# A two-layer graph and feed-forward kernel: rows of two layers turned by transposing transfers instead of TensorE, VectorE's order in the linear layer, and two broadcasts moved

## What is computed

```python
x = x + _L0_gnn_ref(_layernorm(x), edge_weight, L0_gnn_bias, edge_index)       # layer 0: W built from edges; x @ W.T + bias
x = x + _L0_ffn_ref(_layernorm(x)[None], wg, w1, b1, w2, b2)[0]                # 8 experts, 2 for each row
x = x + _L1_gnn_ref(_layernorm(x), edge_index, L1_gnn_W, L1_gnn_b)             # linear layer, then a normalised sum over edges
x = x + _L1_ffn_ref(_layernorm(x)[None], L1_ffn_w1, L1_ffn_w2)[0]              # quantised feed-forward, 4096 hidden
```

## Time and profile before

| what | value |
|---|---|
| median of 3 runs | 1263.97 us |
| the profiled execution | 1262.48 us, of which the span is 1260.5 us |
| layer 0, first to last product | 149.3 to 263.5 us |
| linear layer, first product to last h | 613.4 to 728.9 us |
| TensorE's granted clock over the span | 0.947 of full speed |
| busy share: TensorE, VectorE, ScalarE | 84%, 63%, 38% |

### The profile page before, as it was taken

One profiled execution on the slowest core, in us unless ns is written; L12 is line 12 of the kernel. 1 busy time (PEld: TensorE's weight loads), 2 busy tenths in 40 slices (PEclk: granted clock), 3 DMA queues, 4 the chain that ended last, 5 costly groups with the idle time before them and its releaser, 6 DMA issues.

```text
span 1260.5 us, 20122 instructions
## 1 busy us (share of the span) xinstructions
PE 1063.4 (84%) x7645; PEld 593.5 (47%) x7645; DVE 788.6 (63%) x1082; ACT 481.3 (38%) x552; POOL 163.5 (13%) x215
## 2 busy tenths in 40 slices
PE   1777699974699999982699988888999999999998
PEld 1666344444456555551344444444444444444444
DVE  7998677678255555564677568888837444444431
ACT  3388434443344454451222223433223333333331
POOL 5200323311111110002312001111100000000000
PEclk9898799977699999996799989999999999999999
DMA  4466244363666766643422065666200000000000
GB/s 166 137 247 222 74 159 169 134 230 108 197 230 248 250 249 236 220 167 108 134 67 67 1 199 185 203 198 197 87 1 1 17 18 17 17 17 17 17 17 29
DMA packets 51803, 159.28 MB, mean 126 GB/s; under 512 B 12329, under 2 KB 12651, under 8 KB 47647
## 3 DMA queue, kind: packets, MB, share of 16 engines
q1 hardware_dynamic: 42143, 136.10, 30.8%
q0 software_dynamic: 9600, 22.36, 5.8%
HBM read 137.78 MB, written 20.65 MB: 126 GB/s over the span
## 4 chain that ended last, share of the span: by engine, by line
PE 56%; DVE 20%; issue 9%; DMA 7%; ACT 6%; POOL 1%; DVEq 1%; ACTq 0%; SPq 0%; POOLq 0%
PE ps L1045 11%; PE ps L1070 11%; PE ps L957 8%; PE ps L975 7%; PE ps L864 6%; PE ps L1027 4%; DVE fq L1900 4%; DVE stats L1444 2%; DMA fnat_a<-in_L_ffn_w 2%; DVE xn L1585 2%; DVE x L1848 1%; PE ps L931 1%; ACT xh L1187 1%; DMA gx<-xs_d,tok_i 1%; DVE w1l L1740 1%
## 5 line engine op out<-in xcount | busy, mean ns | idle before, releaser
L1045 PE MATMUL ps<-w1q,xqt 128*128 128x512 fp8e4 x640 | 139.7, 379 | 13.1 <-ACT xqt L1333 13.1
L1070 PE MATMUL ps<-w2q,hqt 128*128 128x512 fp8e4 x640 | 143.0, 379 | 8.7 <-ACT hqt L1342 8.7
L1935 DVE TENSOR_REDUCE hm<-hf 128x1 f32<-128x512 f32 x80 | 54.3, 685 | 93.5 <-ACT hf L1337 93.5
L1045 PEld LDWEIGHTS ps<-w1q,xqt 128*128 128x128 f16 x640 | 61.9, 98 | 87.7 <-issue 14.5
L1070 PEld LDWEIGHTS ps<-w2q,hqt 128*128 128x128 f16 x640 | 61.1, 98 | 78.6 <-issue 10.2
L1337 ACT ACTIVATE hf<-ps,fs 128x512 f32<-128x512 f32 x80 | 54.9, 687 | 91.0 <-PE ps L1045 91.0
L957 PE MATMUL ps<-xdh,w1h 128*128 128x314 f16 x256 | 77.6, 303 | 3.5 <-DVE w1l L1740 2.7
L957 PE MATMUL ps<-xdh,w1l 128*128 128x314 f16 x256 | 77.0, 301 | 0.0
L957 PE MATMUL ps<-xdl,w1h 128*128 128x314 f16 x256 | 76.8, 300 | 0.0
L644 POOL TENSOR_TENSOR rtmp<-mv,consts 128x1 f32<-128x1 f32 x40 | 12.7, 318 | 456.4 <-DVE mv L1449 456.4
L1342 ACT ACTIVATE hqt<-ps 128x1024 f16<-128x1024 f16 x40 | 39.8, 1022 | 68.3 <-PE ps L1052 68.3
(11 more groups left out here) (280 smaller groups left out, 2331.1 us busy)
## 6 DMA issues: line engine op xcount, KB each, us to landing
abs_in<-in_L_ffn_w SPq DMA_DIRECT2D x32, 1024.0 KB, 4.8
wstage<-in_L_ffn_w SPq DMA_DIRECT2D x32, 1024.0 KB, 11.9
fnat_a<-in_L_ffn_w SPq DMA_DIRECT2D x48, 512.0 KB, 4.4
eo_d<-eo SPq DMA_DIRECT2D x16, 512.0 KB
bias_b<-in_L_ffn_w SPq DMA_DIRECT2D x16, 512.0 KB, 4.1
xs_d<-xs_all SPq DMA_DIRECT2D x10, 512.0 KB, 4.3
out_x<-out_t SPq DMA_DIRECT2D x9, 512.0 KB, 2.6
b2b<-in_L_ffn_b SPq DMA_DIRECT2D x8, 512.0 KB
```

What stands on the lines that cost most here:

```text
L1045: last = mm(ps[:, n % 4, :], xqt[:, u, k, :], w1q[:, k, n * 512:(n + 1) * 512], start=(k == 0), stop=(k == KD - 1))
L1070: last = mm(ps[:, 4 + h, :], hqt[:, k, :], w2q[:, k, h * 512:(h + 1) * 512], start=(k == 0), stop=(k == KF - 1))
L1935: last = v.tensor_reduce(hm[:, u, n:n + 1], hf[:, u, n * 512:(n + 1) * 512], AX.X, ALU.max, apply_absolute_value=True)
```

## The change

1. **Turning by transfer.** In layer 0 and the linear layer tiles 2 to 9 (`by_transfer`) are no longer turned by TensorE. SP waits for `xh` and `xl` of the tile and stores both to a buffer in device memory, `xt_d`, in runs of 256 bytes (`rows_out`). Once the product of tile n-2 is done, and both stores and the transposing transfer before have landed, SP issues one transposing transfer of 512 KB into `xt` (`rows_turned`), which holds what were `xth` and `xtl`. TensorE waits for that (`wait_turned`). For these tiles TensorE's 16 transposes, ScalarE's copy `xth` and VectorE's copy `xtl` are gone. The routing stage still turns on TensorE.
2. **Written out.** The loops of these two stages on SP, TensorE, ScalarE and VectorE are written out instead of looped.
3. **VectorE's order in the linear layer.** The rest `hs_l` of tile i-1 now stands in iteration i, after `xn` of tile i+2; the two additions are split around `xl`.
4. **Broadcasts.** The linear layer's `bias_b` is issued before the stores `xs_d`, and no longer beside the last stores of the experts. `b2b` waits until the three gathers of expert 0 have landed; the loads of expert 1's weights stand behind it.

```diff
+        xt_d = nc.dram_tensor("xt_d", [2, 2 * KD * P, P], F16).ap()
...
+        FIRST = 2
+        def by_transfer(n):
+            return not R_MOE <= n < R_LIN1 and n % NT >= FIRST
...
+            def rows_out(n):
+                u = n % 2
+                sp.wait_ge(s_xh, n + 1)
+                sp.wait_ge(s_xl, n + 1)
+                for a, part in enumerate(parts(n, u)):
+                    sp.dma_start(xt_d[u].rearrange("(a k p) c -> a p k c", a=2, p=P)[a],
+                                 part.rearrange("p (k c) -> p k c", c=P)).then_inc(s_xrow, 16)
+            def rows_turned(n):
+                u = n % 2
+                sp.wait_ge(s_mm, n)
+                sp.wait_ge(s_xrow, 32 * moved(n) + 32)
+                if moved(n) > 0:
+                    sp.wait_ge(s_xt, 16 * moved(n))
+                sp.dma_start(xt[:, u, :, :, :].rearrange("p a k c -> p (a k c)"), xt_d[u], transpose=True).then_inc(s_xt, 16)
+            def transfers(r, i):
+                if by_transfer(r + i + 1) and i + 1 < NT:
+                    rows_turned(r + i + 1)
+                if i + 2 < NT:
+                    rows_out(r + i + 2)
...
+            sp.wait_ge(s_biased, NT)
+            sp.dma_start(bias_b[:, :], gb_in.partition_broadcast(P)).then_inc(s_bias, 16)
...
             sp.wait_ge(s_xstore, 16 * NT)
+            for s in range(3):
+                sp.wait_ge(s_g[s], 16)
             sp.dma_start(b2b[:, :], b2_in[0].partition_broadcast(P)).then_inc(s_b2, 16)
...
-            sp.dma_start(bias_b[:, :], gb_in.partition_broadcast(P)).then_inc(s_bias, 16)
+            for i in range(NT):
+                transfers(R_LIN1, i)
...
+            def wait_turned(n):
+                if by_transfer(n):
+                    pe.wait_ge(s_xt, 16 * moved(n) + 16)
+                else:
+                    pe.wait_ge(s_xth, turned(n) + 1)
+                    pe.wait_ge(s_xtl, turned(n) + 1)
...
+                for i in range(NT):
+                    if i + 1 < NT and not by_transfer(r + i + 1):
+                        transposes(r + i + 1, 1 - i % 2)
+                    body(i, i % 2)
...
+                if i + 2 < NT:
+                    norm(R_LIN1, i + 2, u)
+                if i > 0:
+                    rest_of_row(i - 1)
+                if i + 3 < NT:
+                    mixed(i + 3, 0)
+                if i + 2 < NT:
+                    low(R_LIN1 + i + 2, u)
+                if i + 3 < NT:
+                    mixed(i + 3, 1)
+                    mixed_statistics(i + 3)
```

More of the change, by code:

```diff
@@ L492, in _ @@
             sp.dma_start(wg32[:, :, :], wg_in.rearrange("(k p) e -> p k e", p=P)).then_inc(s_wg, 16)
-            with sp.Fori(0, 8) as j:
-                for u in range(2):
-                    sp.wait_ge(s_abs, 2 * j + u + 1)
-                    sp.dma_start(abs_in[:, u, :], f2_pieces[2 * j + u]).then_inc(s_absin[u], 16)
+            def rows_out(n):
[18 more added lines that the diff above has]
+            for i in range(NT):
+                if i < KD:
+                    for u in range(2):
+                        sp.wait_ge(s_abs, 2 * i + u + 1)
+                        sp.dma_start(abs_in[:, u, :], f2_pieces[2 * i + u]).then_inc(s_absin[u], 16)
+                transfers(R_GNN0, i)
             w1v = w1_in.rearrange("e (g k p) h -> e g p k h", g=2, p=P)
@@ L842, in transposes @@
                 pe.wait_ge(s_xh, n + 1)
[L843 to L844 removed]
+                if n > 0:
+                    pe.wait_ge(s_xth, turned(n))
                 for k in range(KD):
@@ L866, in product, with normalised @@
                 last.then_inc(s_mm, 1)
[L868 removed]
+            def normalised(r, body):
                 transposes(r, 0)
[L872 to L877 removed]
+                for i in range(NT):
+                    if i + 1 < NT and not by_transfer(r + i + 1):
+                        transposes(r + i + 1, 1 - i % 2)
+                    body(i, i % 2)
             pe.wait_ge(s_built, 1)
@@ L1602, in normalised @@
                 copy_low(r, 0)
-                def step(i, u):
-                    if not last_of(i, NT):
+                for i in range(NT):
+                    u = i % 2
+                    if i + 1 < NT and not by_transfer(r + i + 1):
                         dve.wait_ge(s_mm, r + i + 1)
                         copy_low(r + i + 1, 1 - u)
-                    if not last_of(i, NT, 2):
+                    if i + 2 < NT:
                         norm(r, i + 2, u)
```

101 lines of the change are left out of this document (56 added, 45 removed).

## The result

The changed kernel takes 1251.6 us at the median of its runs (1248.45 to 1256.98) against 1263.97 us before; the ratio of the two is 0.9894, with a 95% interval of 0.9868 to 0.992. That is 12 us less, inside the range of 1235 to 1263, but only six tenths of the 20 us that were forecast, and 1.6 us outside the forecast's own stretch of 1235 to 1250: it lies where the prediction had put rivals 3 and 2. The profiled executions differ by 1262.48 - 1251.82 = 10.7 us.

What follows compares the result with a forecast made beforehand. Stages of different limits alternate: 56% of the chain TensorE, 20% VectorE, 7% transfers. Terms -10.7 - 2 - 7 - 0.5 = -20.2 us took 1262.5 to 1242.3 as profiled, 1243.8 on the median; forecast 1243 us, range 1235 to 1263.

Steps and rivals of the forecast that it cites:

- rival 3: Third gather before the experts: slow by itself, so only 2 of the 7 us come; 1248 us, chance 0.08.
- rival 2: Layer 0: transfers late behind the loads, period 12.9 us, linear layer keeps its gain; 1257 us, chance 0.15.
- Linear layer, -10.7 predicted: Linear layer: without transposes TensorE becomes the bound at 10.36 us a tile, ending at 718.2 instead of 728.8.
- VectorE's two waits: Linear layer: VectorE waits for ScalarE, 1.59 us for hs_h and 1.12 for xh a tile; both were to go.
- Price of the transfer: Both layers: one transposing transfer of 512 KB was taken to land in 6 us.
- Neither bound: Length of one transposing transfer: at least 4.1 us from small pieces, at most 18.8 us from the mean packet.
- Rival 1: Both layers: transfers longer than a product, slower; 1370 us at 18.8 us each, point of decision about 12; chance 0.17.
- Layer 0, -2 predicted: Layer 0: writing out gives 1.9 us, removed transposes give nothing in the loop; 2 us less in all.
- it just fits: Layer 0: transfer lands about 12 us behind xl, behind two loads, against room of 12.2 us.
- the room of 12.2: Layer 0: longest latency from xl without delay, two VectorE periods less a product, 2 x 11.29 - 10.36.
- b2b and weights behind the gathers, -7 predicted: Third gather of gx: without the broadcasts it lands after the median 7.3 us instead of 14.76, less 0.5.
- bias_b, -0.5 predicted: Experts' last stores: bias_b no longer issued behind them gives 0.5 us, bounds 0 and 2; its new place costs nothing.

Runs made afterwards that it cites:

- the square: Four kernels compared on the linear layer: before 115.7 us, new VectorE order without transfers 111.8, transfers with old order 105.5, both 104.5.
- e3: Changed kernel, all transfers kept, with VectorE's linear-layer order put back as before: 1250.87 us, ratio 0.9903 to before.
- e7: Against e1, each transposing transfer of the linear layer made twice, the second after the first landed: 1268.0 us, ratio 1.0037 to before.
- e1: Changed kernel with layer 0 back on TensorE's transposes, still written out; transfers only in the linear layer: 1246.55 us, ratio 0.9875 to before.
- e6: Changed kernel with b2b issued as before, ahead of the gathers' end, so expert 1's weights early too: 1254.14 us, ratio 0.9942 to before.
- e1 to e3: e1, e3 and, between them, the changed kernel without any transposing transfers, which took 1254.59 us, ratio 0.9928 to before.
- e4: Changed kernel with each expert's third gather of 64 rows instead of 58: 1247.34 us, ratio 0.9877 to before.
- e8: e1 plus e4's gather, and expert results padded so the last stores write 64 rows instead of 58: 1236.83 us, ratio 0.9804 to before.
- e11: Against e8, tile 2's mixture and statistics moved behind the first rows of the linear layer: 1238.54 us, ratio 0.9796 to before.
- e12: Against e11, tile 2 also turned by TensorE, so transfers begin with tile 3: 1231.69 us, ratio 0.9752 to before.
- e9: Changed kernel with only half of each abs_in load in layer 0, leaving out part of the computation: 1246.45 us, ratio 0.988 to before.

## Why the prediction was right, and where it was not

**Linear layer, -10.7 predicted, -11.2 measured.** TensorE is the bound, h to h is 10.36, no transfer is late: each as forecast. The step's reason was only half of it. It put the gain on VectorE's two waits; the square shows that 7.3 us of it are TensorE's own transposes, and that with both waits left in place (e3) the layer is only 1.0 us longer. What the step missed is that the 12.57 us from h to h were not the layer's pace. TensorE before went at 11.26 us a tile and was held to VectorE's pace only in the last three or four, so ten tiles took 115.7. The sum came out right because it was made from the layer's two ends (613.40 and 728.8), not from periods.

**Price of the transfer, 6 us taken; measured 6.0 in the linear layer, 7.5 in layer 0** (medians). A plain one in the same pieces takes 4.3. Neither bound was reached. The Trainium skill (VectorE: DVE Perf Modes, The three transpose paths) has 1309 ns a block, by which 16 blocks in a row would be 20.9 us, an estimate from that page; the rows refute that use of it. The Trainium skill (Advanced Engine Details and Errata, X-Bar Transpose (TRN2)) calls such transfers as fast as plain ones; 4.4 against 4.0 us for the fastest comes near it, 6.0 against 4.3 at the median does not. Rival 1 had its point of decision at 12 us a transfer. No run has a single transfer of that length throughout; e7, with pairs of 10.7 us and the stores behind them, in the linear layer alone, ended at 1.0037 of before.

**Layer 0, -2 predicted, +2.4 measured.** This is the step that failed, at the words "it just fits". Writing out gave 1.5 us (114.3 to 112.8, e1), near the 1.9 forecast. That whatever stands behind the loads lands late was foreseen, and the latency was 11.8 to 12.1 us in five of the seven tiles behind loads, as estimated, but by two errors against each other. The second load took 7.3 to 9.0 us where I had taken 5.1, a median over both loads (before, the second alone took 5.4 to 6.2), and the transfer landed 1.8 to 2.7 us after it where I had some 4. In tile 6 the load took 9.0, the latency was 13.4 us, and the room of 12.2 was passed.

The larger part is a term that the sum did not have, the clock. In tile 3 the latency of 12.1 us did fit: TensorE waited 3.0 us, and at full clock its product would have ended within 0.1 us of the time when x was due. But the granted clock fell behind the wait, the product took 12.2 us where others take 10.5 (both from first start to last end), and x was 1.8 us late. In tile 6 x was 3.8 us late, 2.4 of them by the product's 12.9 us. So 4.1 of the 5.6 us lost are the clock's. e6 shows the same wait without it: TensorE waited 2.8 us for tile 3, the clock stayed at 1.00, and x came after 11.35 us, with no loss. At the end of the layer 1.9 us come back, since there the products follow one another without transposes.

It is rival 2's mechanism at a smaller size: the four profiles with this layer unchanged have 114.4 to 116.7 us, the seven without transfers in it 111.8 to 113.1. So the transfers cost 1.3 to 4.9 us, 2.4 between the means, and could give little, since VectorE's 11.37 us is the pace.

**b2b and weights behind the gathers, -7 predicted, -2.1 measured; rival 3's "only 2 of the 7 us".** Undoing it (e6) costs 3.1 us. What failed is the assumption that without the broadcast the gather would take the median 7.3: with the broadcast gone that gather still takes 9.7 to 11.1 us (10.40 in the changed kernel, 9.69, 11.05 and 10.23 in e1 to e3), and 7.3 was a median over gathers of both sizes; the eight of 58 rows before took 9.1 us and more. The prediction named that case, "58 rows may be spread over few engines", and read the same thing at the last stores (0.18), but gave it a chance of 0.08. The two stand side by side in the same code and have the same 58; they should have been judged alike.

**bias_b, -0.5 predicted; -1.6 for the stage.** The stores went from 7.84 to 7.04 us, inside the bounds of 0 to 2; the other 0.8 us of the stage has no cause shown. In its new place it costs nothing that the stages show.

**Not predicted: the experts, +2.6.** TensorE waits 4.0 us in the last expert for one weight piece of ScalarE (`gwt_h`) where it waited 3.0, and the granted clock falls behind that wait, where it did not before (before, then after):

```profile
550.00:554.00 4.00, 3.30 (x26) 2.16 (x23) 0.00 (x0) 0.63 (x2) 0.00 (x0) 1.00 0.21 83
```

```profile
550.00:554.00 4.00, 4.00 (x22) 2.52 (x20) 0.00 (x0) 0.00 (x0) 0.00 (x0) 0.62 0.21 83
```

Kernels with 64-row gathers (e4, e8, e11, e12) have 240.0 to 241.2 us here, those without 240.7 to 244.5. That the lighter gathers help is likely but wasn't tried by itself, and why the wait is longer in the changed kernel stays open. The terms sum to -1.4 (start) + 2.4 - 2.1 + 2.6 - 1.6 - 11.2 + 0.8 (rest) = -10.5, the spans' difference but for rounding. The -1.4 of the start lies within its scatter: it is 147.8 to 150.3 us in the changed kernel and the twelve made from it. So one step was right in size, three were off by 1 to 5 us, and that the total fell inside the range owes something to its width.

## What to carry to other kernels

A transfer that takes over work from an engine is worth something where that engine sets the stage's pace and the DMA engines have room. Here that held in the linear layer and not in layer 0, where the same edit only added waits. A wait of TensorE can cost more than its length, since the clock may fall behind it. Look at the number of rows of a transfer before its size: 58 rows went over two engines, and six unused rows more made the store three times as fast. When two engines exchange tiles through two buffers, take the pace from the stage's ends, not from the distance of two tiles: a period may be longer than the pace for as long as the lag fits in the buffer, as in e3; in the kernel before it fitted for the first tiles only.

## What the hardware showed unexpectedly

In layer 0 of the changed kernel, TensorE's waits of 3.0 and 4.1 us were each followed by a granted clock at or near the lower level (1.2 GHz) for four us and more; those of up to 1.9 us in e9 were not, nor was one of 3.0 in the last expert before. The length of the wait does not settle it: behind a wait of 2.8 us for tile 3 the product took 12.2 us in e4 and 10.5 in e6. Issuing one transposing transfer held SP's queue for 1.5 to 7.1 us. And transposing transfer, gathers and stores together kept the DMA share above 1 at 81 to 152 GB/s, where layer 0 had 271 GB/s at a share of 0.92.
